# Both gcn passes as bfloat16 products of three table pieces, in a four-layer graph network on one Trainium2 core

## The chip, the cores and the metric

The kernel runs on one core of one Trainium2 chip. The metric is the device time of one execution in microseconds (us). Engines are named as in the profile: PE (matrix products), DVE (VectorE), ACT (ScalarE), POOL (GpSimd), SP (SyncE, which here only starts transfers); an engine name with a q is its instruction queue.

## What is computed

A graph of N = 3125 nodes with 256 features and E = 53125 edges passes four layers, each on relu(layernorm(x)), each added to x. Cut to what matters:

```python
edge_index = jnp.stack([src, dst])
h = jnp.maximum(_layernorm(x), 0.0)
x = x + sage(h, src, dst, edge_weight, w_self, w_neigh)      # weighted sum over edges, 2 products, row norm
h = jnp.maximum(_layernorm(x), 0.0)
x = x + gcn2(h, W1, b1, W2, b2, edge_index)
#   gcn_conv: h = x @ W; deg counts edges into d, loops added; norm = dinv[s] * dinv[d]
#             out = segment_sum(h[s] * norm, d) + b          # 128 wide, then 256 wide
h = jnp.maximum(_layernorm(x), 0.0)
x = x + hops(h, src, dst, edge_weight, W, b)                 # two weighted hops, relu, product
h = jnp.maximum(_layernorm(x), 0.0)
x = x + rgcn2(h, W0, b0, W1, b1, edge_index, edge_type_8)
#   _rgcn_layer: segment_sum(relu((x @ W[r])[edge_type, src] + b), dst), twice, r over 8 relations
```

## The kernel before

Nodes are padded to 25 tiles of 128. Every sum over edges is written as a dense product: POOL scatters the edge records into buckets by (destination tile, source tile), and from the buckets DVE, ACT and PE build, block by block, two dense 3200 x 3200 matrices, one of edge weights and one of edge counts (how many edges go from a node to another). They are stored to DRAM as float32 (`weights_dense`, `counts_dense`). The stages follow one another:

- **sage.** Building the blocks and the first weighted sum run together, tile by tile. A tail of product, row norm, layer norm and the product with W1 follows each tile a few steps later. It ends with `table("gcn1", t)`, 25 tiles of 128 x 128 float32 in `t_sb`, written by ACT. Behind the loop PE counts how many edges were dropped, DVE writes `flag`, and every engine reads it: where it is not zero a general path (skipped here) rebuilds the matrices. All engines branch around that path.
- **gcn1, gcn2, hop1, hop2** (the list `DENSE`). For each of the 25 destination tiles SP loads the row of 25 blocks in two halves (13 and 12 blocks) into a double buffer `stream`, and PE multiplies each 128 x 128 block with the table tile of its source (128 columns wide in the gcn passes, 256 in the hops), summing in one of two PSUM banks `agg`. DVE then makes the row's result: in `gcn1_rows` four operations, the last of which writes `table("gcn2", t)`; in `gcn2_rows` and `gcn2_product` a product with W2 and a layer norm.
- **parting.** The relation layers need the edges sorted into early and late relations. DVE works out the places between rows of gcn1 (`mark_early`, `split_early`, `place_parted`, called by `parting` before the row of an iteration), and the last of these operations writes `pos_u` and signals `s_split`. POOL waits for it and then starts 416 indirect scatters into `edges_parted`, waits until all have landed and signals `s_parted`. SP waits for `s_parted` **between** the loads of hop1 and those of hop2, loads the parted edges back (`kept`), and only then goes on to hop2's blocks.
- **rel1a, rel1b, rel2a, rel2b.** Four passes in which POOL gathers rows by index and PE sums them with one-hot matrices.

SP's queue is in order: a wait in it holds all the loads behind it. Between the loads of gcn1 and gcn2 SP also starts 4 loads of relation biases and 2 of relation weights (1024 KB each). Each of DVE's operations on a row is waited for before the next is started (the helper `Steps`).

Of the kernel before, what the change touches and what calls it, by code (L numbers as in the profile page):

```python
# [40 lines left out]
def build_gnn(nc, x, src, dst, edge_type, edge_weight, w_self, w_neigh, gcn_w1, gcn_b1, gcn_w2,  # L41
# [67 lines left out]
    with ExitStack() as ctx:  # L109
# [9 lines left out]
        def dram(name, shape):  # L119
            return nc.dram_tensor(name, shape, F32).ap()  # L120
# [6 lines left out]
        c_dram = dram("counts_dense", (NPAD, NPAD))  # L127
# [38 lines left out]
        relw = sb("relw", [P, KB, REL, D])  # L166
        y_sb = sb("y_sb", [P, REL, D])
# [33 lines left out]
        relw_flat = relw[:].rearrange("p k r d -> p (k r d)")  # L201
# [6 lines left out]
        before, before_late, edge_no = (gathered[:, k * CHUNKS:(k + 1) * CHUNKS] for k in range(3))  # L208
        split_i, split_hi = (gathered[:, k * CHUNKS:(k + 1) * CHUNKS].bitcast(I32) for k in range(3, 5))
        all_one, chunk_sums, split_f = (gathered[:, k * CHUNKS:(k + 1) * CHUNKS] for k in range(5, 8))  # L210
        pads = gathered[:, 8 * F:8 * F + 2 * RC].rearrange("p (c f) -> p c f", f=2)
# [3 lines left out]
        wraw = y_sb[:].rearrange("p r d -> p (r d)")  # L215
# [4 lines left out]
        c_block = t_sb[:, LANE:2 * LANE]  # L220
# [61 lines left out]
        s_idx = sem("indices_ready")  # L282
# [222 lines left out]

        def load_edges(eng, a, to, done):
# [14 lines left out]
        def _(sp):  # L521
# [7 lines left out]

            sp.wait_ge(s_fill, 6)  # L530
# [9 lines left out]
            load_last(s_x)  # L540

# [31 lines left out]
            def load_biases(b, layer):  # L573
                for j in range(2):
                    sp.dma_start(relb_sb[:, layer, j, :], b.partition_broadcast(P)).then_inc(s_wrel[0], 16)

            sp.wait_ge(s_flag, 1)
            with sp.If(irregular(sp) > 0):
# [15 lines left out]
                sp.wait_ge(g_sum_ready, TILES)  # L594

            for k, n in enumerate(DENSE):
                of = c_dram if n in ("gcn1", "gcn2") else w_dram
                for t in range(TILES):
                    at = TILES * (k + 1) + t
                    for part in range(2):  # L600
                        if n == "gcn1":
                            sp.wait_ge(c_stored[part], 16 * (t + 1))
                        if at - 2 < TILES:
                            sp.wait_ge(w_stored[at % 2][part], 16 * ((at - 2) // 2 + 1))
                        sp.wait_ge((half_free, sum_ready)[part], at - 1)
                        sp.dma_start(half(at, part), dense(of, t, part)).then_inc(s_stream[at % 2][part], 16)
# [1251 lines left out]
```

## Time and profile before

| | us |
|---|---|
| median of 3 runs | 2842.55 |
| the 3 runs | 2839.63, 2842.55, 2846.33 |
| the profiled execution | 2843.29 |
| its span, first to last instruction | 2841.4 |
| PE busy | 2525.3 |
| POOL busy | 1726.6 |
| DVE busy | 1327.8 |

The profiled execution lies 0.7 us above the median and has 1.9 us around its span. The busy times are sums over stages with different limits, so they don't tell what a change in one stage is worth. The rows further down are of single stages.

### The profile page before, as it was taken

Reading aid. Unit: us, or ns where it says so; the run is one execution under the profiler, and the core shown is the slowest. Engines: PE = TensorE matmul, PEld = TensorE weight load, DVE = VectorE, ACT = ScalarE, POOL = GpSimd, SP = SyncE. Lnnn points to the kernel's source line nnn. Section 1 sums busy time; section 2 is a strip of 40 time slices with the busy share of each in tenths; the row PEclk is TensorE's granted clock in tenths of the full one; section 3 lists DMA queues with packets and bytes.
Section 4 is the critical chain, followed back from the end, with each engine's and each line's share of the span. In section 5 each row is a group of like instructions: output and inputs, shape, how many; then the busy total and the mean of one; then the engine's idle time right before and its main releaser. Section 6 shows DMA issues by size and latency. Waiting matters only on the chain.

```text
span 2841.4 us, 44073 instructions
## 1 busy us (share of the span) xinstructions
PE 2525.3 (89%) x12873; PEld 2026.6 (71%) x12874; DVE 1327.8 (47%) x2836; ACT 561.7 (20%) x1659; POOL 1726.6 (61%) x1701
## 2 busy tenths in 40 slices
PE   6799999899898999999999997998788879987675
PEld 4598888788798988888777774665555546555454
DVE  7799988797322551111244233444333424433332
ACT  1355555555100000000011112111011121110000
POOL 5788878772067777774000004777777657777776
PEclk9899999999999999999999998999999989998888
DMA  3133333333698779945444434555454545554343
GB/s 98 50 146 149 151 142 128 121 143 140 207 295 281 241 250 349 314 151 158 134 133 150 134 118 135 161 155 154 133 150 148 148 131 160 155 148 113 115 115 100
DMA packets 208107, 454.85 MB, mean 160 GB/s; under 512 B 52672, under 2 KB 141870, under 8 KB 207818
## 3 DMA queue, kind: packets, MB, share of 16 engines
q1 hardware_dynamic: 56004, 257.55, 26.0%
q0 software_dynamic: 66944, 111.48, 14.9%
q10 hardware_dynamic: 84998, 83.76, 8.7%
q8 instruction: 90, 1.47, 0.2%
q14 instruction: 71, 0.58, 0.1%
HBM read 285.85 MB, written 166.80 MB: 159 GB/s over the span
## 4 chain that ended last, share of the span: by engine, by line
PE 54%; POOL 27%; issue 13%; DMA 3%; DVE 2%; ACT 1%; ACTq 1%; PEldq 0%; DVEq 0%; POOLq 0%; PEld 0%; SPq 0%
PE agg L980 29%; POOL edges_bucketed L665 16%; POOL gathered L720 12%; PE agg L1028 10%; PE y L819 10%; PE prod L804 2%; DMA gathered<-table_rel,idx_rel 1%; DMA edges_bucketed<-edges,pos_u 1%; PE agg L884 1%; ACTq L1259 1%; PE turn_ps L789 0%; ACT turned L1079 0%; PE y L860 0%; DMA table_rel<-y_sb 0%; DVE relw L1494 0%
## 5 line engine op out<-in xcount | busy, mean ns | idle before, releaser
L720 POOL DMA_INDIRECT gathered<-table_rel,idx_rel x840 | 810.6, 965 | 696.5 <-ACTq L1259 443.8
L1028 PE MATMUL agg<-gathered,onehot 128*128 x2464 | 617.1, 407 | 137.5 <-SPq L620 81.6
L1028 PEld LDWEIGHTS agg<-gathered,onehot 128*128 128x128 f32 x2464 | 492.0, 204 | 266.5 <-issue 197.2
L665 POOL DMA_INDIRECT edges_bucketed<-edges,pos_u x416 | 507.0, 1219 | 148.1 <-issue 124.0
L980 PE MATMUL agg<-t_sb,stream 128*128 128x128 f32 (+1 forms) x3750 | 562.8, 312 | 14.6 <-issue 7.6
L980 PEld LDWEIGHTS agg<-t_sb,stream 128*128 128x128 f32 x3750 | 526.2, 193 | 48.4 <-issue 14.8
L1794 DVE SCALAR_TENSOR_TENSOR onehot<-iota,keybase,edges 128x256 f32<-128x256 f32 x616 | 278.1, 483 | 592.2 <-PE agg L1028 482.7
L704 POOL DMA_INDIRECT edges_parted<-parted,pos_u x416 | 402.0, 966 | 180.2 <-issue 126.1
L819 PE MATMUL y<-relw,turned 128*128 128x512 f32 x600 | 283.2, 617 | 74.1 <-ACT turned L1094 41.4
L884 PE MATMUL agg<-h_sb,stream 128*128 128x257 f32 x1250 | 338.5, 396 | 0.0
L860 PE MATMUL y<-gathered,relw 128*128 128x128 f32 x1300 | 238.8, 293 | 41.1 <-DVE t_sb L1511 15.2
L980 PE MATMUL agg<-gathered,stream 128*128 128x256 f32 x1250 | 271.5, 380 | 0.0
L860 PEld LDWEIGHTS y<-gathered,relw 128*128 128x128 f32 x1300 | 218.5, 194 | 72.3 <-ACT t_sb L1171 20.3
L819 PEld LDWEIGHTS y<-relw,turned 128*128 128x128 f32 x600 | 111.2, 195 | 217.6 <-issue 175.5
L980 PEld LDWEIGHTS agg<-gathered,stream 128*128 128x128 f32 x1250 | 238.7, 191 | 32.8
L884 PEld LDWEIGHTS agg<-h_sb,stream 128*128 128x128 f32 x1250 | 217.0, 193 | 21.9 <-issue 0.2
L1154 ACT ACTIVATE gathered<-gathered,recs 128x128 f32<-128x128 f32 x650 | 195.5, 387 | 93.7 <-DVE gathered L1475 93.7
L1113 ACT ACTIVATE y_sb<-y_sb 128x512 f32<-128x512 f32 x200 | 125.7, 629 | 444.1 <-DVE y_sb L1428 387.9
L1079 ACT COPY turned<-turn_ps 128x512 f32<-128x512 f32 (+2 forms) x75 | 30.6, 408 | 840.3 <-PE turn_ps L789 840.1
L1428 DVE TENSOR_TENSOR y_sb<-y,relb_sb 128x512 f32<-128x512 f32 x200 | 129.6, 686 | 87.5 <-PE y L819 67.5
L1494 DVE TENSOR_REDUCE relw<-gathered 128x128 f32<-128x1664 f32 (+2 forms) x50 | 152.2, 3044 | 0.0
L863 PE MATMUL y<-gathered,relw 128*128 128x128 bf16 x650 | 141.0, 223 | 0.0
(198 smaller groups left out, 1740.3 us busy)
## 6 DMA issues: line engine op xcount, KB each, us to landing
table_rel<-y_sb ACTq DMA_DIRECT2D x200, 256.0 KB, 2.9
stream<-counts_dense SPq DMA_DIRECT2D x50, 832.0 KB
stream<-weights_dense SPq DMA_DIRECT2D x50, 832.0 KB
stream<-counts_dense SPq DMA_DIRECT2D x50, 768.0 KB
stream<-weights_dense SPq DMA_DIRECT2D x50, 768.0 KB
table_rel<-zeros ACTq DMA_DIRECT2D x2, 12800.0 KB, 92.6
weights_dense<-stream SPq DMA_DIRECT2D x25, 832.0 KB, 3.4
counts_dense<-t_sb SPq DMA_DIRECT2D x25, 832.0 KB, 5.2
```

The source lines that it names most:

```text
L665: pool.indirect_dma_start(recs_dram, bass.IndirectOffsetOnAxis(ap=pos_u[0:rows, c:c + 1], axis=0), edges[0:rows, c, :], None).then_inc(s_s ...
L704: pool.indirect_dma_start(parted_dram, bass.IndirectOffsetOnAxis(ap=pos_u[:, c:c + 1], axis=0), parted[:, c, :], None).then_inc(s_scat[q % ...
L720: pool.indirect_dma_start(gathered[:, slot * D:(slot + 1) * D], None, tables[n], bass.IndirectOffsetOnAxis(ap=idx_rel[:, c:c + 1], axis=0) ...
L819: mm = pe.matmul(to[:], rows[:, k, :], relw[:, k, 2 * g:2 * g + 2, :], start=(k == 0), stop=(k == KB - 1))
L860: pe.matmul(bank[:, k * D:k * D + P], src_hot[:, h % 2, bucket, :], pair_hot[:, h % 2, bucket, 0, :], start=j == 0, stop=j == len(buckets) ...
L863: mm = pe.matmul(bank[:, k * D + P:(k + 1) * D], upper(src_hot[:, h % 2, bucket, :]), upper(pair_hot[:, h % 2, bucket, 1, :]), start=j == ...
L884: mm = pe.matmul(sums("sage", t)[:, 0:D + 1], stream[:, t % 2, s * P:(s + 1) * P], table("sage", s), start=s == 0, stop=s == TILES - 1, sk ...
L980: mm = pe.matmul(sums(n, t)[:, 0:width], stream[:, at % 2, s * P:(s + 1) * P], table(n, s), start=s == 0, stop=s == TILES - 1)
L1028: mm = pe.matmul(agg[b][:, 0:D], onehot[:, half_ * QUAD + k, :], gathered[:, bass.ds(((q + quads0) & (GQ - 1)) * (QUAD * D) + k * D, D)], ...
L1154: last = nc.scalar.activation(pair_hot[:, h % 2, j, 0, :], pair_hot[:, h % 2, j, 1, :], ACT.Copy, scale=recs[:, t % RECS, c, 2:3])
L1494: nc.vector.tensor_reduce(hot_sum[:, h % 4, :], pair_hot[:, h % 2, 0:count + own, 1, :].rearrange("p b d -> p d b"), AXX, ALU.add).then_in ...
L1794: nc.vector.scalar_tensor_tensor(onehot[:, at:at + 2, :], iota[:].unsqueeze(1).broadcast_to([P, 2, P]), keybase[:, bass.ds(t + late * TILE ...
```

## The change

Both gcn passes compute the same sums with bfloat16 operands. The counts are small whole numbers, exact in bfloat16, so `counts_dense` is now stored and loaded as bfloat16 (the general path keeps a float32 copy, `counts_whole`). Each float32 table tile is split into three bfloat16 pieces that add up to it (`split_rows`: cast, subtract, cast, subtract). PE multiplies a count block with all three pieces side by side, 384 columns in one instruction, and DVE adds the three partial sums (`add_pieces`). The first table is split in groups of 5 tiles: four groups inside the sage tail and the fifth after the branch on `flag`; the second is split row by row in `gcn1_rows`. Around this, the biases of the relation layers are loaded at the start, the relation weights after hop1's block loads (their memory now holds the pieces of gcn2 before), and the three steps of the parting move from iterations 0, 6, 8 to 3, 7, 9.

```diff
+            def stream_blocks(n, of, to):
+                for t in range(TILES):
+                    at = TILES * (DENSE.index(n) + 1) + t
+                    for part in range(2):
...
+                        sp.wait_ge((half_free, sum_ready)[part], at - 1)
+                        sp.dma_start(to(at, part), dense(of, t, part)).then_inc(s_stream[at % 2][part], 16)
 
             sp.wait_ge(s_flag, 1)
             with sp.If(irregular(sp) > 0):
...
+                for n in DENSE[:2]:
+                    stream_blocks(n, c_whole, half)
+            with sp.Else():
+                for n in DENSE[:2]:
+                    stream_blocks(n, c_dram, half_counts)
+
+            for n in DENSE[2:]:
+                stream_blocks(n, w_dram, half)
+                if n == "hop1":
                     load_relations(sp, rel_w0, 0, REL, s_wrel[0])
-                if n == "hop1":
                     sp.wait_ge(s_parted, 1)
                     sp.dma_start(kept, parted_dram.rearrange("(p c) f -> p c f", p=P)).then_inc(s_kept, 16)
...
+                            if t == 0 and n == "gcn1" and split:
+                                pe.wait_ge(s_pieces, s // 5 + 1)
...
+                            if split:
+                                mm = pe.matmul(sums(n, t)[:, 0:3 * HID], half_counts(at, part)[:, place],
+                                               pieces[n][:, s, :, :].rearrange("p k d -> p (k d)"),
+                                               start=s == 0, stop=s == TILES - 1)
...
+            def split_rows(n, step, tiles):
...
+                step(nc.vector.tensor_copy(first, rows))
+                step(nc.vector.tensor_tensor(rest, rows, first, ALU.subtract))
+                step(nc.vector.tensor_copy(second, rest))
+                step(nc.vector.tensor_tensor(third, rest, second, ALU.subtract))
+
+            def split_first(group, step):
+                dve.wait_ge(S["sage", "table_ready"], min(5 * group + 5, TILES))
+                split_rows("gcn1", step, slice(5 * group, 5 * group + 5))
+                dve.sem_inc(s_pieces, 1)
...
+            SPLITS = {2 * TILES + 2: (0,), 2 * TILES + 4: (1,), 2 * TILES + 5: (2, 3)}
...
+                if i in SPLITS:
+                    for group in SPLITS[i]:
+                        split_first(group, prep)
...
             step = Steps(dve, s_dense, 0, 0)
+            split_first(4, step)
+
+            def add_pieces(n, t):
+                step(nc.vector.tensor_tensor(post[:, 0:HID], sums(n, t)[:, 0:HID], table(n, t), ALU.add))
+                for k in (1, 2):
+                    step(nc.vector.tensor_tensor(post[:, 0:HID], sums(n, t)[:, k * HID:(k + 1) * HID], post[:, 0:HID],
+                                                 ALU.add))
...
             def parting(t, b):
-                if t == 0:
+                if t == 3:
                     mark_early()
-                if t == 6:
+                if t == 7:
                     split_early()
-                if t == 8:
+                if t == 9:
                     place_parted()
```

On DVE at the end of the sage tail, before: the last tile's update and norm, then the flag.

```order
L1449 TENSOR_SCALAR small<-small 128x1
L1450 RECIPROCAL small<-small 128x1
L1451 SCALAR_TENSOR_TENSOR x_sb<-prod,small,x_sb 128x256
L1398 BN_STATS bnst<-x_sb 128x6
L1399 BN_AGGR small<-bnst 128x2
L1403 RECIPROCAL small<-small 128x1
L1404 TENSOR_SCALAR post2n<-x_sb,small 128x256
L1405 TENSOR_SCALAR normed<-post2n,small 128x256
L1560 TENSOR_SCALAR flag<-y 128x1
```

The same place on DVE in the changed kernel, from the last tile's BN_AGGR on. L1558 to L1561 are the four steps of a split, 5 tiles at once.

```order
L1437 BN_AGGR small<-bnst 128x2
L1558 CAST gathered<-t_sb 128x5x128
L1559 TENSOR_TENSOR gathered<-t_sb,gathered 128x640
L1560 CAST gathered<-gathered 128x5x128
L1561 TENSOR_TENSOR gathered<-gathered 128x5x128
L1441 RECIPROCAL small<-small 128x1
L1442 TENSOR_SCALAR post2n<-x_sb,small 128x256
L1443 TENSOR_SCALAR normed<-post2n,small 128x256
L1558 CAST gathered<-t_sb 128x5x128
L1559 TENSOR_TENSOR gathered<-t_sb,gathered 128x640
L1560 CAST gathered<-gathered 128x5x128
L1561 TENSOR_TENSOR gathered<-gathered 128x5x128
```

One split has come ahead of the last norm, and two behind it (the second with the same four rows again) ahead of the flag; another stands before the norm of tile 23.

On DVE in gcn1, the row before the one with `place_parted`'s last step, of the changed kernel (before, L1641, L1643, L1644 and L1645 stood here, one each):

```order
L1694 TENSOR_TENSOR post<-agg0,t_sb 128x128
L1696 TENSOR_TENSOR post<-agg0,post 128x128 x2
L1709 TENSOR_SCALAR post<-post,dinv 128x128
L1710 TENSOR_TENSOR post<-post,b1_sb 128x128
L1711 TENSOR_SCALAR t_sb<-post,dinv 128x128
L1558 CAST rel_sb<-t_sb 128x128
L1559 TENSOR_TENSOR gathered<-t_sb,rel_sb 128x128
L1560 CAST rel_sb<-gathered 128x128
L1561 TENSOR_TENSOR rel_sb<-gathered,rel_sb 128x128
```

A row has gone from four operations to ten.

## Rows read from the trace of the kernel before

**Rows 1.** By stretch: length, PE, PEld, DVE, ACT, POOL busy, clock, DMA share, GB/s
```profile
742.00:893.00 151.00, 143.09 (x1252) 142.84 (x1252) 38.87 (x121) 0.00 (x0) 76.77 (x80) 0.96 0.92 298
893.00:1066.30 173.30, 162.72 (x1325) 155.29 (x1326) 81.42 (x241) 13.62 (x49) 131.88 (x137) 0.98 0.77 246
1066.30:1337.60 271.30, 271.30 (x1251) 238.54 (x1250) 41.87 (x106) 0.30 (x1) 193.31 (x201) 0.99 0.74 248
```
**Rows 2.** Timeline of SP between hop1's and hop2's loads: start, length
```profile
1321.86 0.33 SPq L613 DMA_DIRECT2D edges<-edges_parted  x1
1322.23 50.16 SPq L606 DMA_DIRECT2D stream<-weights_dense  x10
```
**Rows 3.** Waits of SP: total us, times, longest
```profile
SPq L613 <- POOLq L709: 5.2, 1, 5.2
```
**Rows 4.** POOL's parting scatters: all, the first and the last of 416
```profile
L704 POOL DMA_INDIRECT edges_parted<-parted,pos_u x416: 955/962/1191, 792.2 to 1319.6; - x139
792.16 1.07 POOL L704 DMA_INDIRECT edges_parted<-parted,pos_u  x1 [53.83 <-DVE pos_u L1739]
1319.57 0.96 POOL L704 DMA_INDIRECT edges_parted<-parted,pos_u  x1 [0.30 <-issue]
```
**Rows 5.** Timeline of PE: gcn1, two tiles of gcn2, start of hop2
```profile
742.50 19.91 PE L980 MATMUL agg<-t_sb,stream 128*128 128x128 f32 x150 [7.06 <-DMA stream<-counts_dense]
762.42 0.34 PE L972 MATMUL y<-onehot,ones_b 128*128 128x416 bf16 x1
762.59 122.99 PE L980 MATMUL agg<-t_sb,stream 128*128 128x128 f32 x1100
908.25 5.74 PE L980 MATMUL agg<-t_sb,stream 128*128 128x128 f32 x50
915.00 5.75 PE L980 MATMUL agg<-t_sb,stream 128*128 128x128 f32 x50
1337.69 21.75 PE L980 MATMUL agg<-t_sb,stream 128*128 128x256 f32 x100
```
**Rows 6.** Timeline of DVE: end of the sage tail, the flag, the first step of gcn1
```profile
727.33 0.18 DVE L1399 BATCH_NORM_AGGREGATE small<-bnst 128x2 f32<-128x6 f32 x1
735.48 0.16 DVE L1560 TENSOR_SCALAR flag<-y 128x1 int32<-128x1 f32 x1 [2.04 <-PE y L915]
740.25 0.53 DVE L1705 TENSOR_SCALAR onehot<-edges 128x416 bf16<-128x416 f32 x1 [4.62 <-issue]
```
**Rows 7.** Timeline of SP after the flag: gcn1's first loads
```profile
736.99 3.30 SPq L606 DMA_DIRECT2D stream<-counts_dense  x4
```
**Rows 8.** Timeline of DVE in gcn1: mark_early's last step, a row, split_early, place_parted
```profile
742.79 0.41 DVE L1711 MEMSET gathered<- 128x416 f32 x1 [0.15 <-DVE parted L1709]
751.78 0.29 DVE L1643 TENSOR_SCALAR post<-post,dinv 128x128 f32<-128x128 f32 x1
752.10 0.29 DVE L1644 TENSOR_TENSOR post<-post,b_sb 128x128 f32<-128x128 f32 x1
775.56 1.02 DVE L1716 TENSOR_TENSOR_SCAN gathered<-gathered,y 128x416 f32<-128x416 f32 x1 [0.22 <-DVE t_sb L1645]
778.98 0.65 DVE L1727 SCALAR_TENSOR_TENSOR gathered<-gathered,late_at 128x416 f32<-128x416 f32 x1
786.65 0.59 DVE L1731 TENSOR_TENSOR gathered<-gathered 128x416 f32<-128x416 f32 x1
791.01 0.38 DVE L1739 CAST pos_u<-gathered 128x416 uint32<-128x416 f32 x1
```
**Rows 9.** By stretch, as rows 1: the start of gcn1
```profile
742.00:748.00 6.00, 5.50 (x26) 5.53 (x27) 1.04 (x2) 0.00 (x0) 0.00 (x0) 0.50 1.00 380
```
**Rows 10.** POOL's scatters of the sage stage, one of them beside DVE; durations min/median/max
```profile
L665 POOL DMA_INDIRECT edges_bucketed<-edges,pos_u x416: 955/962/2674, 28.1 to 659.1; - x139
640.23 1.94 DVE L1475 TENSOR_TENSOR relw<-iota,local 128x1536 f32<-128x1536 f32 x2
640.44 2.37 POOL L665 DMA_INDIRECT edges_bucketed<-edges,pos_u  x1 [0.30 <-issue]
```

More of the change, by code:

```diff
@@ L594, in _ @@
                 sp.wait_ge(g_sum_ready, TILES)
[L596 to L606, printed above, removed]
-                if n == "gcn1":
-                    load_biases(rel_b0, 0)
-                    load_biases(rel_b1, 1)
+                for n in DENSE[:2]:
[6 more added lines that the diff above has]
+                if n == "hop1":
                     load_relations(sp, rel_w0, 0, REL, s_wrel[0])
-                if n == "hop1":
                     sp.wait_ge(s_parted, 1)
@@ L914, in _, with gcn @@
+            def gcn(split):
+                static_tiles(dense_visits("gcn1", split), [])
+                pe.sem_inc(S["gcn2", "product_free"], 1)
+                pe.sem_inc(S["gcn2", "rows_turned"], 1)
+                static_tiles(dense_visits("gcn2", split),
+                             [(1, lambda t, b: turn("gcn2", halves[0:1], t)),
+                              (1, lambda t, b: rows_product("gcn2", t, [w2_sb[:]]))])
             pe.wait_ge(s_drops, 1)
@@ L1006, in _ @@
                      "rel2b": []}
-            for n in DENSE:
-                if n in ("gcn2", "hop2"):
+            for n in ("hop1", "hop2"):
+                if n == "hop2":
                     pe.sem_inc(S[n, "product_free"], 1)
                     pe.sem_inc(S[n, "rows_turned"], 1)
-                if n == "hop2":
                     pe.sem_inc(y_added, 4)
@@ L1512, in evict @@
                                       ).then_inc(evicted[1], 1)
+            def split_rows(n, step, tiles):
+                rows = t_sb[:, LANE * DENSE.index(n):LANE * (DENSE.index(n) + 1)].rearrange(
+                    "p (t d) -> p t d", d=HID)[:, tiles, :]
+                first, second, third = (pieces[n][:, tiles, k, :] for k in range(3))
+                rest = remains[n].rearrange("p (t d) -> p t d", d=HID)
+                step(nc.vector.tensor_copy(first, rows))
[6 more added lines that the diff above has]
+                dve.sem_inc(s_pieces, 1)
             for what in ("src", "dst", "sum"):
                 onehots(0, what)
+            SPLITS = {2 * TILES + 2: (0,), 2 * TILES + 4: (1,), 2 * TILES + 5: (2, 3)}
             for i in range(2 * (TILES - 1) + 9):
```

112 lines of the change are left out of this document (67 added, 45 removed).

## The prediction

> **What bounds the kernel now.** I read the busy time by stretch first. In gcn1 and in hop1 PE is busy nearly throughout (143 of 151 us, 271.3 of 271.3), in gcn2 for 163 of 173 [rows 1]. Read alone, this says that a faster product in the gcn passes shortens the kernel. The second view must be SP's timeline, since SP's queue is in order: it loads the parted edges at 1321.86 and the first block of hop2 only at 1322.23 [rows 2], after a wait of 5.2 us for POOL [rows 3]. So POOL's parting is already last at that place, and hop2 escapes only because its first product starts at 1337.69 [rows 5], 15.5 us after SP may load for it. The third view, POOL's scatters, shows that this chain can't be compressed: 416 scatters start between 792.16 and 1319.57, 527.4 us, 1.27 us each, in the thick of transfers and after them [rows 4]. It starts with the write of `pos_u`, which ends at 791.39 [rows 8]; the first scatter follows 0.77 us later. The path that will set hop2's start is therefore: flag, gcn1's first rows on DVE, `pos_u`, 416 scatters, edges loaded back, hop2's first blocks. The two gcn products beyond tile 8 aren't on it.
>
> **PE in the gcn passes, removed.** A float32 block costs two records; 1100 take 122.99 us, so 0.224 us a block, 5.6 us a tile [rows 5]. A bfloat16 product with 416 columns takes 0.17 us from its start to the next start (762.42 to 762.59) [rows 5]; scaled to 384 columns 0.16 us (an estimate), so 4.1 us a tile: 1.5 us x 25 = 38 us less in gcn1. In gcn2 a tile takes 6.75 us (908.25 to 915.00) [rows 5]. It can come down by those 1.5 us at best and by nothing at worst, because DVE's row grows by two adds in a loop that PE and DVE go round together; I take 6.0, midway, so 18 us less. The idle stretch between gcn1 and gcn2 (about 7.5 of the 151 us [rows 1] have no product) goes too, since the relation loads no longer stand ahead of gcn2's. In all hop1 would end some 60 us earlier. All of it is worth only what the chain of POOL leaves.
>
> **DVE in the sage tail, added.** A split is two casts and two subtractions over 640 columns. From the 128-column subtraction (0.29 us) and the 416-column one (0.59) [rows 8] a column costs 1.04 ns and the start 0.16, so 0.82 us. A cast of 416 took 0.38 [rows 8], at half the slope: 0.49 for 640; if it were as slow as a subtraction, 0.82. With 0.03 between steps (751.78 plus 0.29 to 752.10 [rows 8]) a group takes 2.8 us, at most 3.4. Four groups stand between the BN_AGGR of tile 23, ending at 727.51 [rows 6], and the flag. Going through DVE's queue: split (2.8), norm and drop count (1.4), last update (2.3), split (2.8), norm (0.9), two splits (5.5) end at 743.3. PE's part of the flag is done by then, so the flag comes at 743.3, not 735.48 [rows 6]: **+7.8 us**, all waits of DVE on ACT and PE already used up.
>
> The Trainium skill weighs on one term here. VectorE: DVE Perf Modes, section "Mode 2×_2P", says that a float32 copy from SBUF runs at two elements per cycle only if the outermost dimension is even, or odd and equal on both sides. The casts write 5 x 128 from a source that may count as 640. The 416-column row agrees with a double rate, but no row has a dimension of 5; by the slow rate the flag would come 2.6 us later still.
>
> **Behind the flag.** SP starts gcn1's first load 1.35 us after the flag is written (735.64 to 736.99) [rows 6, 7]. It now jumps over a longer general path (155 rows of its order, before 54). DVE, which jumps over some 560, took 4.6 us [rows 6]. So the price is between 0 and 3.2 us; I take 1.6. The first product came 5.5 us after the load's start [rows 5, 7]; half as many bytes make it between 2.7 and 5.5, I take 4.1. gcn1's first product then starts at 743.5 + 1.35 + 1.6 + 4.1 = **750.6**, before 742.50. The fifth group is split by about 751 and is needed at product 20: hidden, at up to 4 us later too.
>
> **DVE in gcn1.** The first 6 us ran at a granted clock of 0.50, that is 1.2 GHz, after the 7.06 us that PE had waited [rows 5, 9], so the first tile takes 4.1 + 3 = 7.1 us. A row goes from four steps to ten: eight operations of 0.29, two casts of 0.22 (by the slope above), gaps of 0.03 and the signals, together 3.2 to 3.3 us. It fits in PE's 4.1 us, but the parting steps are extra: `mark_early` before row 2 (740.25 to 743.20, 2.9 us), `split_early` before row 6 (775.56 to 779.63, 4.1 us) and `place_parted` after row 7 (786.65 to 791.39, 4.7 us) [rows 6, 8]. Followed through the queue, rows 2 to 7 run without a break, and `pos_u` is written 46.4 us after gcn1's first product, before 48.9. Rows are shorter on PE, but there is one more of them ahead and each is longer on DVE. So `pos_u` comes at 797.0, POOL starts at 797.8 (before 792.16): **+5.6 us**.
>
> **POOL and SP.** The last scatter starts 527.4 us later at 1325.2. Then as before 2.3 us until SP loads the edges and 0.4 until hop2's first block [rows 2, 4]. The first block took 5.5 us to arrive in gcn1's case [rows 5, 7], with the edges' 420 KB ahead of it perhaps 1.2 more: hop2 starts at **1334.6**, before 1337.69: 3.1 us earlier. But PE will have been idle for some 55 us and starts at 1.2 GHz; if for 6 us as in [rows 9], that gives back 3.0. Sum 0. DVE's additional subtractions beside POOL's scatters (rival 1) I put at 0.6. What follows hop2's start isn't touched. The relation weights load during the idle time, the biases early, long before their use: 0 for both, hidden by 20 us and more.
>
> Against the profiled execution's own 2843.3 this gives 2843.9; that execution lies 0.7 us above the median of the three. I predict 2844.0.
>
> **Rivals.**
> 1. *DVE slows POOL's scatters* (slower). In the sage stage the same scatter has a median of 0.962 us but one of 2.37 lies beside 1.94 us of TENSOR_TENSOR on DVE, and 416 of them take 631 us where the parting takes 527 [rows 4, 10]: 104 us more. The Trainium skill has the mechanism, GPSIMD Engine Reference, section "Specifications": the SBUF interfaces are shared with VectorE, with contention where an instruction has two SBUF inputs or a 2-port mode. If each of the 100 half-tile comparisons of 1.9 us like the one shown has its share, 104 us are lost in 190, 0.55 us per us. The change adds, from POOL's start to gcn1's end, 14 rows of two subtractions and two casts, 1.0 us each row: 14 us, 8 us lost at that rate, so 2851. Against it: short operations of this kind run beside the parting scatters already, and their median is the minimum plus 7 ns [rows 4]. It decides the sign from 4 us lost. Chance 0.12.
> 2. *The flag or the jump comes later still*: slow casts (+2.6) and the full jump (+1.6), with a late first block, 2849. Chance 0.06.
> 3. *The tail absorbs the splits*: the flag isn't later, the block comes sooner, gcn1 starts at 741, 9.6 us before my estimate: 2834. Against it: 11 us of work on a queue with about 3 us of gaps. Chance 0.07.
> 4. *The gain of PE comes through*: hop2 follows hop1 at once. gcn1 750.6 + 105, gcn2 + 151, hop1 + 271.3 = 1278, 60 us earlier: 2784. It needs POOL to make its scatters at 1.14 us instead of 1.27, which no stretch of [rows 4] shows, whatever else ran. Chance 0.03.
>
> **How the numbers follow.** The sum above has 0.72. Its own range comes from the bounds: casts 0 to +2.6, jump -1.6 to +1.6, blocks -1.4 to +1.4, clock -3 to +1, splits or rows up to 2 shorter: 2837 to 2850. For 8 in 10 I reach to 2836 and to 2853, which takes in rival 1. 0.2% is about 5.7 us, what a measurement of this kernel can tell from no change: faster means under 2836.9, slower over 2848.2. Faster: rivals 3 and 4, 0.10. Slower: rivals 1 and 2, 0.18. The same: 0.72.
>
> **What the profile after would show.** Products of 384 columns 0.16 us apart in gcn1 and tiles of 4.1 us; the flag near 743; gcn1's first product near 751; `pos_u` near 797; 416 scatters at the same pace with the last near 1325; hop1 ending near 1278; then a gap on PE of about 55 us that SP's wait for POOL explains; hop2's first product near 1335 at a clock of 0.50. I am wrong if hop2 starts far from 1335: earlier, if POOL's pace changes or `pos_u` comes sooner; later, if the median of POOL's scatters leaves 0.96 us, or if anything but POOL ends PE's gap.

## The result, and the profile after

| | before | after |
|---|---|---|
| median of 20 runs each, us | 2843.07 | 2848.17 |
| lowest and highest | 2837.05, 2846.33 | 2845.15, 2853.18 |
| profiled execution, its span | 2843.29, 2841.4 | 2853.18, 2851.4 |

The ratio is 1.002 with a 95% interval of 1.0013 to 1.0026: 3.7 to 7.4 us slower, which is at the edge of what counts as the same here. The profiled execution of the changed kernel is the longest of its 20 runs, so its span says 10.0 us more where the medians say 5.1. I therefore read distances inside a stage, not absolute times.

By stretch, columns as in rows 1, the changed kernel (gcn1, gcn2, hop1, the first 6 us of hop2 and the 2 us after):

```profile
759.00:870.00 111.00, 106.42 (x632) 62.76 (x633) 79.04 (x265) 0.00 (x0) 48.31 (x50) 0.96 0.69 191
869.30:1028.00 158.70, 127.57 (x703) 72.52 (x701) 100.69 (x302) 13.61 (x49) 120.57 (x126) 0.99 0.52 146
1028.00:1300.50 272.50, 272.47 (x1251) 239.06 (x1249) 40.38 (x105) 0.29 (x1) 207.09 (x215) 0.99 0.72 244
1341.00:1347.00 6.00, 5.45 (x13) 4.41 (x14) 0.00 (x0) 0.00 (x0) 0.00 (x0) 0.50 0.85 356
1347.00:1349.00 2.00, 2.00 (x11) 1.74 (x10) 0.00 (x0) 0.00 (x0) 0.00 (x0) 0.96 0.00 0
```

Against [rows 1], gcn1 has gone from 151 us to 109.5 (759.80 to the next stretch) and gcn2 from 173.3 to 158.7; hop1 takes 1 us more. From the start of gcn1's first product to that of hop1's last it takes 540.3 us, before 595.0. Those 55 us have come back as a start of gcn1 that is 17.3 us later and as one gap, in PE's timeline of the changed kernel (start, length, idle before):

```profile
759.80 22.26 PE L957 MATMUL agg<-gathered,stream 128*128 128x384 bf16 x125 [13.78 <-DMA stream<-counts_dense]
795.33 8.30 PE L957 MATMUL agg<-gathered,stream 128*128 128x384 bf16 x50 [0.73 <-DVEq L1708]
806.68 62.79 PE L957 MATMUL agg<-gathered,stream 128*128 128x384 bf16 x375 [3.05 <-DVEq L1708]
1289.73 10.74 PE L961 MATMUL agg<-gathered,stream 128*128 128x256 f32 x49
1341.55 24.59 PE L961 MATMUL agg<-t_sb,stream 128*128 128x256 f32 x100 [41.08 <-issue]
```

hop1 ends at 1300.5, and hop2 starts 41.1 us later, at 1341.55; it was 1337.69 [rows 5]. The releaser of the gap is given as "issue", which names nobody. SP's timeline and waits, and POOL's scatters, show what PE waits for:

```profile
1279.29 1.29 SPq L530 DMA_DIRECT2D rel_sb<-in_L_gnn_W  x2
1335.76 0.34 SPq L632 DMA_DIRECT2D edges<-edges_parted  x1
1336.14 1.97 SPq L601 DMA_DIRECT2D stream<-weights_dense  x4
```
```profile
SPq L632 <- POOLq L728: 55.2, 1, 55.2
```
```profile
L723 POOL DMA_INDIRECT edges_parted<-parted,pos_u x416: 957/962/1128, 806.5 to 1333.5; - x139
806.49 1.01 POOL L723 DMA_INDIRECT edges_parted<-parted,pos_u  x1 [53.09 <-DVE pos_u L1806]
1333.48 0.96 POOL L723 DMA_INDIRECT edges_parted<-parted,pos_u  x1 [0.30 <-issue]
```

SP's wait of 5.2 us for POOL [rows 3] has become 55.2. It begins when SP is done with the relation weights (1279.29 plus 1.29) and stands ahead of hop2's loads, which follow the edges 0.4 us later, as in [rows 2]. The scatters take 527.0 us from the first to the last, before 527.4 [rows 4]; they only begin 14.3 us later, 4.3 of which were there at the end of sage already (tile 23's BN_AGGR). The other 10.1 us arise here, in DVE's and SP's timeline of the changed kernel from that operation to gcn1's first load:

```profile
731.59 0.18 DVE L1437 BATCH_NORM_AGGREGATE small<-bnst 128x2 f32<-128x6 f32 x1
731.68 0.79 DVE L1558 CAST gathered<-t_sb 128x640 bf16<-128x640 f32 x1
732.51 0.83 DVE L1559 TENSOR_TENSOR gathered<-t_sb,gathered 128x640 f32<-128x640 f32 x1
733.37 0.82 DVE L1560 CAST gathered<-gathered 128x640 bf16<-128x640 f32 x1
734.22 0.83 DVE L1561 TENSOR_TENSOR gathered<-gathered 128x640 bf16<-128x640 f32 x1
...
747.00 0.82 DVE L1558 CAST gathered<-t_sb 128x640 bf16<-128x640 f32 x1
...
750.55 0.16 DVE L1618 TENSOR_SCALAR flag<-y 128x1 int32<-128x1 f32 x1
755.59 0.82 DVE L1558 CAST gathered<-t_sb 128x640 bf16<-128x640 f32 x1 [4.89 <-issue]
...
805.34 0.38 DVE L1806 CAST pos_u<-h_sb 128x416 uint32<-128x416 f32 x1
```
```profile
754.89 2.91 SPq L601 DMA_DIRECT2D stream<-counts_dense  x4
```

The last line of DVE is the end of `place_parted`. A cast of 640 columns takes as long as a subtraction, 0.8 us. The flag has no idle time before it any more (2.04 us before, [rows 6]): DVE's queue decides when it comes. And SP starts 4.18 us after the flag is written (750.71 to 754.89) instead of 1.35.

### The profile page after: what moved, and what is told of

The parts are those of the page before. It is cut to its first block, busy times and chain, and to the rows that moved or that the text cites. A ratio compares the mean times of both kernels' runs of the same rounds, so it can differ in the third digit from the quotient of the medians.

```text
span 2851.4 us, 41798 instructions
## 1 busy us (share of the span) xinstructions
PE 2458.0 (86%) x11623; PEld 1868.1 (66%) x11624; DVE 1401.9 (49%) x3056; ACT 561.9 (20%) x1659; POOL 1732.6 (61%) x1701
## 3 DMA queue, kind: packets, MB, share of 16 engines
q8 instruction: 81, 1.33, 0.2%
## 4 chain that ended last, share of the span: by engine, by line
PE 44%; POOL 29%; issue 15%; DVE 6%; DMA 3%; ACT 1%; ACTq 1%; DVEq 0%; PEldq 0%; POOLq 0%; PEld 0%; SPq 0%
PE agg L961 19%; POOL edges_bucketed L684 15%; POOL gathered L739 14%; PE y L838 10%; PE agg L1066 8%; PE agg L957 3%; PE prod L823 2%; DMA edges_bucketed<-edges,pos_u 1%; DMA gathered<-table_rel,idx_rel 1%; ACTq L1297 1%; PE agg L903 1%; DVE post L1696 1%; PE turn_ps L808 1%; DVE bnst L1436 0%; DVE gathered L1733 0%
## 5 line engine op out<-in xcount | busy, mean ns | idle before, releaser
L684 POOL DMA_INDIRECT edges_bucketed<-edges,pos_u x416 | 509.9, 1226 | 148.6 <-issue 123.4
L838 PE MATMUL y<-rel_sb,turned 128*128 128x512 f32 x600 | 284.6, 619 | 74.3 <-ACT turned L1132 40.4
L961 PE MATMUL agg<-t_sb,stream 128*128 128x256 f32 x1250 | 276.5, 382 | 41.1 <-issue 41.1
L961 PEld LDWEIGHTS agg<-t_sb,stream 128*128 128x128 f32 x1250 | 239.4, 192 | 74.5 <-issue 41.4
L879 PE MATMUL y<-gathered,rel_sb 128*128 128x128 f32 x1300 | 239.3, 293 | 44.6 <-DVE t_sb L1549 17.8
L879 PEld LDWEIGHTS y<-gathered,rel_sb 128*128 128x128 f32 x1300 | 218.6, 194 | 76.4 <-DVE t_sb L1549 21.0
L838 PEld LDWEIGHTS y<-rel_sb,turned 128*128 128x128 f32 x600 | 111.6, 196 | 218.6 <-issue 176.4
L1151 ACT ACTIVATE rel_sb<-rel_sb 128x512 f32<-128x512 f32 x200 | 125.8, 629 | 444.0 <-DVE rel_sb L1466 387.7
L1466 DVE TENSOR_TENSOR rel_sb<-y,relb_sb 128x512 f32<-128x512 f32 x200 | 129.7, 687 | 88.7 <-PE y L838 68.5
L1532 DVE TENSOR_REDUCE rel_sb<-gathered 128x128 f32<-128x1664 f32 (+2 forms) x50 | 152.2, 3044 | 0.0
L882 PE MATMUL y<-gathered,rel_sb 128*128 128x128 bf16 x650 | 141.1, 223 | 0.0
```

Of the source, the lines that this page charges most:

```text
L684: pool.indirect_dma_start(recs_dram, bass.IndirectOffsetOnAxis(ap=pos_u[0:rows, c:c + 1], axis=0), edges[0:rows, c, :], None).then_inc(s_s ...
L838: mm = pe.matmul(to[:], rows[:, k, :], relw[:, k, 2 * g:2 * g + 2, :], start=(k == 0), stop=(k == KB - 1))
L879: pe.matmul(bank[:, k * D:k * D + P], src_hot[:, h % 2, bucket, :], pair_hot[:, h % 2, bucket, 0, :], start=j == 0, stop=j == len(buckets) ...
L882: mm = pe.matmul(bank[:, k * D + P:(k + 1) * D], upper(src_hot[:, h % 2, bucket, :]), upper(pair_hot[:, h % 2, bucket, 1, :]), start=j == ...
L961: mm = pe.matmul(sums(n, t)[:, 0:width], half(at, part)[:, place], table(n, s), start=s == 0, stop=s == TILES - 1)
L1532: nc.vector.tensor_reduce(hot_sum[:, h % 4, :], pair_hot[:, h % 2, 0:count + own, 1, :].rearrange("p b d -> p d b"), AXX, ALU.add).then_in ...
```

## The experiments

**What these chips are.** The twelve experiments ran on four chips, and on all four every kernel takes far longer than above: the kernel before 4195 to 4209 us at the median, the changed one 4143. Where most of the 1300 us are is shown below and told at the end. On these chips POOL's chain doesn't bind, so their total times can't repeat the verdict. What they can settle is the distances inside a stage, and what happens once POOL's scatters are taken out. For the changed kernel the distances in the table below agree with the first chip to 0.01 us in A, 0.5 in D and 0.8 in E (after_again); B and C spread by 1 to 2 us. All times are medians; the ratio is to the kernel before on the same chip.

| kernel | us | ratio, 95% |
|---|---|---|
| after_again (the changed kernel) | 4143.0 | 0.985 (0.982 to 0.988) |
| e1_parting_first | 4151.4 | 0.985 (0.981 to 0.989) |
| f1_parting_first (the same again) | 4128.8 | 0.981 (0.973 to 0.988) |
| e2_before_parting_first | 4225.3 | 1.003 (1.000 to 1.006) |
| e3_splits_behind_flag | 4150.9 | 0.984 (0.979 to 0.988) |
| e4_short_jump | 4131.4 | 0.979 (0.974 to 0.983) |
| e5_short_ops | 4133.2 | 0.981 (0.978 to 0.985) |
| e6_long_ops | 4141.5 | 0.985 (0.981 to 0.989) |
| e7_parting_before_sage | 4149.8 | 0.987 (0.983 to 0.990) |
| f7_parting_before_sage (the same again) | 4135.2 | 0.982 (0.976 to 0.988) |
| g1_after_no_scatters | 4190.0 | 0.997 (0.993 to 1.000) |
| g2_before_no_scatters | 4229.6 | 1.006 (1.003 to 1.010) |

And the chain in parts, from the traces: A, from the end of tile 23's BN_AGGR to the flag's start; B, from the flag's end to gcn1's first load on SP; C, from there to gcn1's first product; D, from there to the end of `pos_u`'s write; E, from A's start to the first parting scatter (us).

| kernel | A | B | C | D | E |
|---|---|---|---|---|---|
| before (first chip) | 7.96 | 1.35 | 5.51 | 48.89 | 64.65 |
| after (first chip) | 18.78 | 4.18 | 4.92 | 45.92 | 74.73 |
| after_again | 18.77 | 4.93 | 3.92 | 45.38 | 73.94 |
| e3_splits_behind_flag | 8.67 | 4.95 | 4.18 | 56.58 | 75.31 |
| e4_short_jump | 18.76 | 1.34 | 4.20 | 46.69 | 71.94 |
| e1_parting_first | 18.77 | 3.83 | 5.81 | 11.74 | 41.09 |
| f1_parting_first | 18.78 | 4.29 | 5.33 | 12.04 | 41.38 |
| e2_before_parting_first | 8.41 | 1.35 | 5.59 | 15.56 | 31.85 |

**after_again**: the changed kernel, nothing edited.

> The changed kernel once more, unchanged, on the chip of the three runs beside it, as their yardstick: near 2848, with hop2's first product some 582 us behind gcn1's first.

Measured: 64.8 us faster than before on the same chip, so neither the expected time nor the 582 us came (1070.1). gcn1 is the reason. Its tiles take 4.1 us for the first dozen (a few of them up to 7.3), then eight of them take 67 to 70 us each, then 4.1 again. By stretch, and PE's and POOL's timeline inside the stretch:

```profile
1224.00:1869.00 645.00, 163.89 (x625) 64.79 (x626) 78.00 (x263) 0.00 (x0) 424.72 (x416) 0.56 0.13 34
1310.00:1340.00 30.00, 5.27 (x11) 1.15 (x11) 0.00 (x0) 0.00 (x0) 22.89 (x24) 0.50 0.07 15
1852.00:1869.00 17.00, 16.99 (x95) 9.55 (x94) 12.02 (x44) 0.00 (x0) 0.00 (x0) 0.91 0.70 205
```
```profile
1339.49 0.48 PE L957 MATMUL agg<-gathered,stream 128*128 128x384 bf16 x1 [2.32 <-issue]
1342.30 0.48 PE L957 MATMUL agg<-gathered,stream 128*128 128x384 bf16 x1 [2.33 <-issue]
1345.09 0.48 PE L957 MATMUL agg<-gathered,stream 128*128 128x384 bf16 x1 [2.31 <-issue]
```
```profile
1341.46 0.96 POOL L723 DMA_INDIRECT edges_parted<-parted,pos_u  x1 [0.30 <-issue]
1342.72 0.96 POOL L723 DMA_INDIRECT edges_parted<-parted,pos_u  x1 [0.30 <-issue]
L723 POOL DMA_INDIRECT edges_parted<-parted,pos_u x416: 954/959/1908, 1270.6 to 1825.6; - x139
```

PE makes one product every 2.8 us with no releaser, where it could make one in 0.16. The 2.8 is also the mean over a whole tile, in which PE stands still for 19 us once and then makes seven products in a row. DVE and the transfers are mostly idle with it, while POOL scatters at nearly its usual pace (1.33 us each, 1.27 on the first chip). The slow products begin some 28 us after the first parting scatter and end 9 us after the last, at 1834.4; PE is back at its pace at 1850.9. So on these chips hop1's last product starts at 2294.3, 469 us after the last scatter, and hop2 follows 0.2 us later: there is no gap for PE's gain to vanish in.

**e1_parting_first** puts the three steps of the parting, and the count that PE makes for them, at the head of gcn1; f1 is the same kernel again, on another chip.

```diff
-                    if n == "gcn1" and t == 5:
+                    if n == "gcn1" and t == 0:
                         pe.wait_ge(s_early, 5)
...
-                if t == 3:
+                if t == 0:
                     mark_early()
-                if t == 7:
+                if t == 1:
                     split_early()
-                if t == 9:
                     place_parted()
```

> The changed kernel with the parting's steps in iterations 0 and 1 of gcn1 instead of 3, 7 and 9, all else alike. Theory A (hop2 starts when POOL's 416 scatters have landed, and so at a fixed distance behind the write of pos_u): pos_u is written some 28 us sooner after gcn1's first product (46 us after it in the changed kernel, about 18 here), PE in gcn1 loses up to 5 us to DVE, which its idle time ahead of hop2 (41 us) hides, and the kernel is 25 to 29 us faster than the changed one: about 2820. Rival B (the time is lost in the passes themselves, to DVE's longer rows or to contention, and not in the wait for POOL): no gain, or 5 us slower, 2848 to 2853.

> The changed kernel with the three parting steps at the head of gcn1: mark_early ahead of row 0, split_early and place_parted ahead of row 1. Nothing of the computation is left out. Theory (hop2 starts a fixed 536 us after pos_u is written): pos_u is written some 14 to 20 us after gcn1's first product instead of 46, so POOL starts 26 to 32 us sooner, hop2 starts as much sooner and PE's gap before it falls from 41 us to about 12; with the kernel before at 2843 and the changed one at 2848 the time is 2816 to 2823. Rival (gcn1's rows wait for DVE and the loss there is as large): gcn1 becomes longer by what is won, and the time is 2840 to 2850.

Measured: `pos_u` is written 11.7 and 12.0 us after gcn1's first product instead of 45.4, and POOL starts 33 us sooner (E). The total isn't told apart from after_again's, as it can't be where POOL doesn't bind. The distance is what the theory said. What the 33 us are worth was not measured where POOL does bind; some 30 us is an estimate, from E and the gap of 41.1 on the first chip.

**e2_before_parting_first** does the same to the kernel before.

```diff
-                    if n == "gcn1" and t == 3:
+                    if n == "gcn1" and t == 0:
                         pe.wait_ge(s_early, 5)
...
-                if t == 6:
+                if t == 1:
                     split_early()
-                if t == 8:
                     place_parted()
```

> The same on the kernel before: mark_early in iteration 0 as it was, split_early and place_parted in iteration 1 instead of 6 and 8. Theory A: there hop2 follows hop1 at once with 15 us to spare between the end of the scatters and its first product, so moving the scatters 25 us ahead gives nothing: 2843, within 3 us. Rival B' (POOL's parting already held something back in the kernel before): faster by 5 us or more.

Measured: E falls from 64.65 to 31.85, and the time is that of before or a little more. In the kernel before, too, it is the place of the steps in DVE's queue that sets POOL's start. From gcn1's first product to hop2's it takes 1142.8 us here, the changed kernel 1070.1. This trace also shows what the slow stretch counts by, in PE's timeline beside the scatters:

```profile
1412.63 0.37 PE L980 MATMUL agg<-t_sb,stream 128*128 128x128 f32 x1 [2.43 <-issue]
```

A record of the float32 product comes every 2.8 us too, though it is shorter (0.37 us against 0.48): a tile of 50 records takes 140.0 us, one of 25 takes 70.0 in after_again. So the loss goes by the number of instructions, not by their size. Some 200 of them fall into the stretch in either kernel, eight tiles of the changed one and four of the kernel before. This is 32 us of PE's usual work against 22, an estimate from 4.06 and 5.58 us a tile, so some 10 us of the changed kernel's lead on these chips come from the slow stretch itself.

**e3_splits_behind_flag** takes the four groups out of the tail and puts all five behind the branch.

```diff
-            SPLITS = {2 * TILES + 2: (0,), 2 * TILES + 4: (1,), 2 * TILES + 5: (2, 3)}
+            SPLITS = {}
...
-            split_first(4, step)
+            for group in range(5):
+                split_first(group, step)
```

> The changed kernel with all five groups of the first table split behind the branch on the flag, none in the sage tail. Theory A with the tail as its first cost: the flag is written about 11 us sooner (within 1 us of where it stood before, seen from the end of tile 23's statistics), five splits of 3.4 us follow the branch, products wait for them, and the first row of gcn1 is ready 3 to 5 us sooner than in the changed kernel; pos_u and the end move by the same 3 to 5 us: about 2844. Rival C (the splits were hidden in the tail, the flag waits for PE anyway): the first row comes 10 us later and the kernel takes about 2857.

Measured: A is 8.67, so the splits cost the flag 10.1 us; D is 11.2 us longer than after_again's, and POOL starts 1.4 us later all the same (E). Neither theory came: gcn1's first product starts 17.9 us after tile 23's BN_AGGR instead of 27.8, but its first tile then waits for the splits (15.0 us instead of 5.3). So the sum of the first row is ready 0.2 us sooner, not 3 to 5, and `pos_u` no sooner at all. The splits lie on DVE's path to `pos_u` wherever they stand. In this tail the flag waits 2.7 us for PE, so 10.1 of the 13.6 us of splitting come out at the flag and the rest is that wait and DVE's short ones on ACT:

```profile
1199.17 0.16 DVE L1618 TENSOR_SCALAR flag<-y 128x1 int32<-128x1 f32 x1 [2.74 <-PE y L975]
```

**e4_short_jump** leaves the gcn blocks of the general path out of SP's program; the general path isn't taken on this data.

```diff
-                for n in DENSE[:2]:
-                    stream_blocks(n, c_whole, half)
             with sp.Else():
```

> The changed kernel with the block loads of the general path left out on SP (a path that isn't taken here; it would not work in this kernel), so that SP jumps over 54 rows of its order instead of 155. The way from the flag's write to gcn1's first load was 1.35 us before and 4.2 us in the changed kernel. If the length of the jump is the reason, it is back near 1.4 us and the kernel about 2.8 us faster than the changed one, near 2845. If the reason is another one (the order of the waits ahead of the first load), it stays at 4 us and the time at 2848.

Measured: SP's first load comes 1.34 us behind the flag, as in the kernel before (1.35), where the ten traces with the long path have 3.5 to 5.0. POOL starts 2.0 us sooner than in after_again. The branch itself and its other side are still there, so the length of the skipped code is what costs SP 2.2 to 3.6 us. Flag and load in this trace:

```profile
1216.44 0.16 DVE L1616 TENSOR_SCALAR flag<-y 128x1 int32<-128x1 f32 x1
1217.94 2.54 SPq L601 DMA_DIRECT2D stream<-counts_dense  x4
```

**e5_short_ops and e6_long_ops** add work to DVE in 20 rows of hop1, to see whether it slows POOL's scatters: 24 two-input operations of 128 columns a row in e5, 4 of 1536 columns a row in e6. The edit of e6:

```diff
                 dve.sem_inc(S["hop1", "table_ready"], 1)
+                if t < 20:
+                    for _ in range(4):
+                        step(nc.vector.tensor_tensor(rel_sb[:, 0:12 * P].rearrange("p (k d) -> p k d", d=P),
+                                                     iota[:].unsqueeze(1).broadcast_to([P, 12, P]),
+                                                     ident[:].unsqueeze(1).broadcast_to([P, 12, P]), ALU.add))
```

> The changed kernel with 24 more TENSOR_TENSORs of 128 columns and two SBUF inputs (0.29 us each) behind each of the first 20 rows of hop1 on DVE, 139 us of them in all, beside POOL's scatters; their result is used by nothing and DVE has the time. Theory A with short operations harmless: the scatters keep their pace (527 us from first to last), the time stays within 2 us of the changed kernel's. Rival 1 (DVE with two SBUF inputs stalls POOL at the rate of the sage stage, 0.55 us per us): the scatters take 76 us more, and the kernel takes 2924.

> As the run with short operations, but with 4 TENSOR_TENSORs of 1536 columns (about 1.75 us each) behind each of the first 20 rows of hop1, 140 us in all. Here the sage stage's rate should show whatever the short ones do: the scatters take some 40 to 76 us more, the kernel 2888 to 2924. If it stays at 2848, POOL's slow scatters in the sage stage have another reason than DVE.

Measured: nothing of the question. hop1 began at 2021 and 2019 us, after the last scatter (1821), so the added operations never stood beside one. Both are inconclusive.

**e7_parting_before_sage** works the places out before sage and scatters right behind the buckets' scatters; f7 is the same kernel again. Cut to its core:

```diff
+            mark_early()
+            split_early()
+            place_parted()
             for what in ("src", "dst", "sum"):
                 onehots(0, what)
...
-            static_tiles(None, [(0, parting), (1, gcn1_rows)])
+            static_tiles(None, [(1, gcn1_rows)])
```

> The changed kernel with the whole parting ahead: its steps on DVE, its count on PE and its pads before the sage loop, POOL's 416 scatters directly behind the 416 of the buckets (at about 663 us, done by 1192), other scratch memory for them; the general path, which isn't taken, would not sort again. Theory A: nothing waits for POOL before hop2 any more, hop2 follows hop1 at once, the 41 us of PE's gap, 3 us of slow clock and 4 us of DVE in gcn1 go: 2795 to 2803. This is then the gain that the products themselves bring. Rival D: the scatters collide with the tail of sage and with gcn1, or the steps ahead of sage delay the whole stage by their 15 us: 2810 to 2820.

> The changed kernel with the whole parting taken out of gcn1's rows: DVE works out the places before the sage stage, and POOL makes the 416 parting scatters right behind those of the buckets, near 660 to 1190 us, before it even waits for the flag. Nothing of the computation is left out. Theory (the chain flag, pos_u, 416 scatters sets hop2's start, and PE's gain is only held back by it): SP no longer waits for POOL when hop1's blocks are loaded, hop2's first product follows hop1's last with no gap and at the full clock, near 1300 us instead of 1341.5; with the kernel before at 2843 and the changed one at 2848 the time is 2795 to 2810. Rival (the gap before hop2 is loads or the clock, not POOL): the gap stays and the time is 2840 or more. Rival (DVE's long comparisons in sage slow the extra scatters and the stage with them): the flag comes later by more than 10 us and eats part of the gain: 2815 to 2830.

Measured: neither total is below after_again's beyond its interval. The trace says why. Inside the gcn passes everything the theory said is there: gcn1's first product to hop2's first takes 528.9 us in f7 with no gap (1070.1 in after_again). But the slow stretch has moved with the scatters, into sage, whose first two tiles now take 369 and 173 us instead of 23. By stretch, f7, beside the scatters and in the gcn passes:

```profile
640.00:1170.00 530.00, 70.28 (x208) 47.05 (x208) 28.83 (x39) 18.95 (x63) 407.30 (x385) 0.51 0.04 8
1771.80:2300.50 528.70, 501.69 (x2575) 372.40 (x2576) 202.91 (x647) 13.90 (x50) 0.00 (x0) 0.99 0.65 213
```

208 products in 530 us beside the scatters, 2575 in as long without them.

**g1_after_no_scatters and g2_before_no_scatters** leave the 416 parting scatters out of the changed kernel and of the kernel before; SP's later waits that counted them are lowered to match. The relation layers then read padding in place of edges, in as many instructions: this part of the computation is left out.

```diff
             pool.wait_ge(s_split, 1)
-            for q in range(QUADS):
...
-                    pool.indirect_dma_start(
-                        parted_dram, bass.IndirectOffsetOnAxis(ap=pos_u[:, c:c + 1], axis=0),
-                        parted[:, c, :], None).then_inc(s_scat[q % GQ], 16)
-            for k in range(GQ):
-                pool.wait_ge(s_scat[k], 2 * ROUNDS * 16 * QUAD)
             pool.sem_inc(s_parted, 1)
```

> The changed kernel without the 416 parting scatters: POOL signals the parted edges as soon as their places are worked out, so the relation layers read a prefilled list of padding records in place of the edges; this part of the computation is left out, the number of instructions behind it is not. Theory on a chip where the kernel before needs about 4205 us (nearly nothing of the other engines' new code is carried out while scatters run back to back): the stretch of about 535 us in gcn1 goes away, a tile of gcn1 takes 4.1 us from the first to the last, and the time is 3590 to 3625. Rival (that stretch comes from the transfers of gcn1 or from its new code, not from the scatters): it stays, and the time is over 4090. On a chip where the kernel before needs 2843 the theory is that PE's gap before hop2 goes, 41 us at most: 2800 to 2812.

> The kernel before without the 416 parting scatters, left out in the same way as in the kernel beside it, with which this one is compared: it gives what the change is worth once POOL's chain sets nothing. From gcn1's first product to hop1's last the normal profiles have 595 us before and 540 after, and the flag and the first block come 12 to 15 us later after: so I expect this kernel 38 to 46 us above the changed one without scatters, 3630 to 3670 on a chip where the kernel before needs about 4205 us, and 2840 to 2846, no faster than with its scatters, where it needs 2843. Rival (most of the 55 us don't come through even then, since DMA or DVE holds the gcn passes): the two are within 20 us of one another.

By stretch, gcn1, gcn2 and hop1 of g1, then of g2:

```profile
1211.00:1320.00 109.00, 104.39 (x627) 61.83 (x628) 78.24 (x264) 0.00 (x0) 0.00 (x0) 0.97 0.67 197
1320.00:1474.00 154.00, 127.22 (x701) 72.24 (x700) 95.66 (x301) 13.58 (x49) 0.00 (x0) 1.00 0.50 149
1474.00:1746.50 272.50, 272.50 (x1252) 239.38 (x1251) 40.60 (x106) 0.29 (x1) 0.00 (x0) 0.99 0.72 254
```
```profile
1205.00:1353.00 148.00, 141.76 (x1252) 141.51 (x1252) 37.70 (x121) 0.00 (x0) 0.00 (x0) 0.98 0.91 299
1353.00:1526.80 173.80, 162.78 (x1325) 155.25 (x1326) 78.73 (x242) 13.62 (x49) 0.00 (x0) 0.98 0.75 247
1526.80:1797.80 271.00, 271.00 (x1251) 238.38 (x1250) 40.24 (x105) 0.29 (x1) 0.00 (x0) 1.00 0.70 247
```

Measured: the slow stretch is gone from gcn1. From its first product to hop2's first it takes 534.8 us in g1 and 592.7 in g2, and hop2 follows hop1 within 0.3 us in both: with POOL out of the way PE's gain comes through, 57.9 us. The totals differ by 39.5 us, inside the 38 to 46 expected. In these two traces the later flag and the later first product cost the changed kernel 11.9 us (27.7 against 15.8 us from tile 23's BN_AGGR), which leaves 46.0; the other 6.5 aren't assigned. The absolute totals were wrong by over 550 us: hop2 begins 548 us sooner than in after_again, but from there to PE's last product it is 2423 us instead of 1838. SP waits 1351 us of them for gathered rows. Every padding record asks for the same row, unlike the edges, which may be why; I didn't try it apart. The rival of that expectation is refuted by the stage, not by the total.

## Why the prediction was right, and where it was off

**What bounds the kernel.** Right, and the step on which the rest depends. SP's in-order wait for POOL's parting sets hop2's start in the changed kernel: 55.2 us of wait, first load 0.4 us behind it. That PE's gain is real is shown by g1 and g2 (57.9 us), and by the first chip's trace, where hop1 starts 38 us sooner and hop2 3.9 later. That POOL's chain is what holds it back there rests on this trace, SP's wait above all: no run took the scatters out or moved them on that chip. Rival 4, the gain coming through, is what those chips show where the scatters end long before hop1; on the first chip it was worth nothing.

**PE in the gcn passes.** Products 0.16 us apart and tiles of 4.1, as predicted. The stages were put too short: gcn1 109.5 us for 105 (PE waits 3.8 us for DVE's rows around the parting steps), gcn2 158.7 for 151 (6.3 us a tile, not 6.0). Together with the later start this makes the gap 41 us instead of 55. It cost nothing, since it is time before a wait: an error of 12 us went unpunished because it stood off the path.

**DVE in the sage tail.** The mis-sized term. +7.8 us were predicted; A rose by 10.8. Of the two bounds for the casts the slow one was true: 0.79 to 0.82 us at 640 columns, so 8 casts at 0.82 instead of 0.49 are 2.6 of the 3.0 us missing. VectorE: DVE Perf Modes, section "Mode 2×_2P", of the Trainium skill, on which that doubt was built, gave the right warning: the trace agrees with the slow rate that it allows for 5 tiles at once. It isn't the bfloat16 result or the size alone: in the same trace a cast of one tile (128 columns) to bfloat16 takes 0.23 us where a subtraction takes 0.29, and a cast of 416 columns 0.38. The profile writes the cast's shape as 640 columns, flat, so no row shows that the odd dimension is the cause, and a cast of an even number of tiles wasn't tried.

**Behind the flag.** The jump cost 2.8 us, not 1.6, near the upper bound of 3.2; e4 shows that it is the length of the skipped path. The block came after 4.9 us, not 4.1, within its bounds. gcn1's first product stood 750.6 in the prediction and came at 759.80: 4.3 of that is sage ending later in this execution, 3.0 the tail, 1.2 the jump, 0.8 the block.

**DVE in gcn1.** Right: `pos_u` 45.9 us after the first product (46.4 predicted). e3 shows what the sum took for granted, that the splits are on DVE's path to `pos_u` on either side of the flag.

**POOL and SP.** The scatters' pace is the same to 0.4 us, and the edges load 2.3 us behind the last one, as before. hop2's first product comes 8.1 us behind the last scatter instead of 9.4, and runs at 0.50 for 6 us, as predicted. From tile 23's BN_AGGR to hop2's first product it is 609.8 us against 610.2 before; the low clock then makes hop2's last product 2.9 us later, 6.7 in all with sage's 4.3 (1718.5 against 1711.8). So the terms as measured give +2.4, where I had +0.6. The errors partly cancel: tail, jump and block took 4.9 us more than predicted, the steps up to `pos_u`, the scatters and the load behind them 2.2 us less, and rival 1's 0.6 didn't come.

**Rival 1** is refuted on the first chip: beside the scatters DVE is busy for 187 us instead of 143, and their median is 962 ns in both traces and the time from the first to the last 527.0 us, before 527.4. **Rival 3** too: of 13.6 us of splits the tail took up 2.8, what the prediction gave it. **Rival 2** happened in part: slow casts (+2.6) and most of the jump (+1.2). They are the largest part of what the sum missed, but not all of the distance between forecast and time, as "What stays open" says.

**What was luck.** The forecast of 2844.0 doesn't follow from its own sum: the +0.6 was added to the profiled execution and the 0.7 us by which that execution lies above the median was not taken off, which would have given 2843.2. The measured 2848.17 lies 0.03 us under the 2848.2 that the prediction had set as the bound of slower. And had the bounds been added up, the range would have begun at 2836, not at 2837. That the kernel gains nothing was foreseen by its mechanism; that 5.1 us more still counts as the same was close.

**What stays open.** The medians differ by 5.1 us and the terms explain 2.4. The profiled executions also differ by 4.3 us in sage and 3.3 behind hop2, but these are single executions of kernels that spread by 8 and 9 us. On the other chips sage takes the same from its first product to its last, 571.5 us in after_again and 571.1 in e2. So 2.7 of the 5.1 us aren't assigned.

## What to carry to other kernels

Before speeding up a stage, look for the in-order wait behind it: here SP's queue holds hop2's loads until POOL's chain ends, so 55 us less in the gcn passes became a gap of 41 us and 4 us of delay, and every us added ahead of that chain (casts in the tail, a longer skipped path) made it longer. Work the chain that remains from its first link: the experiments say that the parting steps at the head of gcn1 let POOL start 33 us sooner, and that is the edit to try together with this one. When a price hangs on a rate that may change with the shape, as that of a cast, take the slow bound unless a row of the same shape shows the fast one.

## What the runs showed of the hardware that I hadn't expected

- **Four chips on which PE nearly stops beside POOL's scatters.** The same kernels took 4143 to 4209 us instead of 2848 and 2843. While POOL's indirect scatters run back to back there, PE makes one product in 2.8 us with nothing to wait for, whether it is a float32 record of 128 columns or a bfloat16 one of 384. In after_again 535 us of gcn1 are lost that way and, by the same pattern, about as much at the start of sage (first block product at 620 us instead of 127). From hop2's start to PE's last product it is 1838 us instead of 1504, with POOL's gathers, indirect transfers too, throughout. g1 shows the scatters as the cause in gcn1, f7 that the loss moves with them. What they take from the other engines isn't shown; the delivery of instructions would fit, since no releaser is shown and the price goes by the instruction. Nor is it shown that the chips are what differs: it may be something else that changed after the first measurement.
- **Scatters and comparisons.** In after_again the 416 scatters of the buckets end before sage's first product (28.4 to 596.3 us, mean 974 ns), and sage then takes 571 us. On the first chip they run beside it (28.7 to 662.5, mean 1226 ns) and it takes 600. By these numbers each slows the other, though the chips may differ in more.
- **A branch costs SP by what it skips**: from the flag's write to SP's first load, 1.34 to 1.35 us past 54 rows and 3.5 to 5.0 past 155. Only these two lengths were tried.
